# A gated attention and FFN block on one core: a rewritten opening, and h's first block maxima taken in the down stage

## What is computed

```python
def _quant_act(x2d, reorder_index, select_num):
    g = jnp.maximum(jnp.max(jnp.abs(x2d)) / GSCALE_DIV, 1e-08)
    xr = (x2d / g)[:, reorder_index]
    ...
    normal = _fp8_block_qdq(xr[:, :n])
    ...
    q1 = _fp8_block_qdq(outl)
    q2 = _fp8_block_qdq(outl - q1)
    return jnp.concatenate([normal, q1, q2], axis=1), g
def _L0_ffn_ref(x, w_gate, w_up, w_down, ri_in, ri_mid):
    A, g = _quant_act(x2, ri_in, SELECT)
    ...
    gate = A @ Wg.T * g
    up = A @ Wu.T * g
    h = jax.nn.silu(gate) * up
    Am, gm = _quant_act(h, ri_mid, SELECT)
    return Am @ Wd.T * gm
x = x + jnp.tanh(g_xattn[0]) * _L0_xattn_ref(_layernorm(x, axis=-1), ctx_4096, L0_xattn_x1_scale, L0_xattn_x1_zp, L0_xattn_x2_scale, L0_xattn_x2_zp)
x = x + jnp.tanh(g_ffn[0]) * _L0_ffn_ref(_layernorm(x, axis=-1), L0_ffn_w_gate, L0_ffn_w_up, L0_ffn_w_down, L0_ffn_ri_in, L0_ffn_ri_mid)
```

## Time and profile before

| what | us |
|---|---|
| median of 3 runs | 818.54 |
| the profiled execution's own time | 818.77 |
| its span, first to last instruction | 817.0 |
| PE busy in the span | 731.0 |
| DVE / ACT / POOL busy | 556.3 / 311.3 / 343.7 |
| loop and down stage on the chain that ended last | 387.38 + 224.48 |

### The profile page before, as it was taken

How to read it: one execution, slowest core, us unless ns; L and a number is a source line. 1 busy time by engine, 2 the same in 40 slices (tenths; PEclk the granted TensorE clock), 3 DMA queues, 4 the chain that set the end, 5 groups by cost and what they waited for, 6 DMA issues and landing times.

```text
span 817.0 us, 10350 instructions
## 1 busy us (share of the span) xinstructions
PE 731.0 (89%) x3473; PEld 334.5 (41%) x3473; DVE 556.3 (68%) x957; ACT 311.3 (38%) x382; POOL 343.7 (42%) x206
## 2 busy tenths in 40 slices
PE   0599003999999999999999999999999999999998
PEld 0144002545444444444444444444444444444443
DVE  5459789894475756675757575745898888988800
ACT  2798972445252524343434343430222122121100
POOL 1536766769374747584848575740000000000000
PEclk9989655999999999999999999999999999999999
DMA  8910598339588897979697969774265654555320
GB/s 308 353 60 14 166 279 147 80 64 190 145 173 212 187 211 174 223 169 227 145 232 163 231 163 236 157 157 164 49 152 162 182 129 149 132 161 121 88 60 26
DMA packets 228884, 131.56 MB, mean 161 GB/s; under 512 B 201712, under 2 KB 212976, under 8 KB 227824
## 3 DMA queue, kind: packets, MB, share of 16 engines
q1 hardware_dynamic: 228848, 131.12, 65.2%
HBM read 61.88 MB, written 19.66 MB: 100 GB/s over the span
## 4 chain that ended last, share of the span: by engine, by line
PE 78%; DVE 5%; POOL 5%; DMA 5%; ACT 3%; SPq 2%; issue 1%; DVEq 0%
PE acc L1276 47%; PE acc L1330 27%; DMA big<-in_ctx_dram 3%; PE acc L1223 2%; POOL big L739 1%; POOL h_in L734 1%; DVE big L1535 1%; ACT wbuf_all L919 1%; POOL wbuf_all L715 1%; POOL wbuf_all L708 1%; POOL big L728 1%; DMA wbuf_all<-in_L_ffn_w_up_dram 1%; SPq L455 1%; DMA mid<-big 1%; DMA x_d<-big 1%
## 5 line engine op out<-in xcount | busy, mean ns | idle before, releaser
L1276 PE MATMUL acc<-mid 128*128 128x512 f16 x1920 | 415.1, 379 | 0.0
L1276 PEld LDWEIGHTS acc<-mid 128*128 128x128 f16 x1920 | 187.9, 98 | 226.1
L1330 PE MATMUL acc<-big,mid 128*128 128x512 f16 x1040 | 224.6, 379 | 0.0
L818 POOL TENSOR_TENSOR h_in<-wbuf_all,h_in 128x1024 f16<-128x1024 f32 (+1 forms) x56 | 114.4, 2044 | 97.2 <-ACT h_in L1115 97.1
L1330 PEld LDWEIGHTS acc<-big,mid 128*128 128x128 f16 x1040 | 101.8, 98 | 122.7
L708 POOL TENSOR_TENSOR wbuf_all<-wbuf_all,w_inv 128x1024 f32<-128x1024 f32 (+1 forms) x67 | 125.2, 1873 | 43.6 <-DVE w_inv L1448 43.6
L1558 DVE SCALAR_TENSOR_TENSOR h_out<-acc,gs,silu 128x256 f32<-128x256 f32 (+1 forms) x88 | 41.5, 471 | 102.6 <-ACT silu L956 65.3
L1442 DVE TENSOR_REDUCE tb<-wbuf_all 128x64 f32<-128x1024 f32 (+1 forms) x67 | 78.9, 1178 | 47.3 <-DMA wbuf_all<-in_L_ffn_w_gate_dram 22.2
L912 ACT ACTIVATE wbuf_all<-wbuf_all 128x1024 f32<-128x1024 f32 (+1 forms) x67 | 68.1, 1016 | 82.2 <-POOL wbuf_all L708 81.4
L1115 ACT ACTIVATE h_in<-wbuf_all 128x1024 f16<-128x1024 f32 (+1 forms) x56 | 56.9, 1016 | 103.1 <-DVE wbuf_all L1454 103.1
L1454 DVE SCALAR_TENSOR_TENSOR wbuf_all<-wbuf_all,tb 128x1024 f32<-128x1024 f32 (+1 forms) x56 | 65.1, 1163 | 0.3 <-issue 0.2
(11 more groups left out here) (159 smaller groups left out, 555.0 us busy)
## 6 DMA issues: line engine op xcount, KB each, us to landing
h_in<-h_d SPq DMA_DIRECT2D x8, 1376.0 KB, 7.0
wbuf_all<-in_L_ffn_w_gate_dram SPq DMA_DIRECT2D x21, 512.0 KB, 4.3
wbuf_all<-in_L_ffn_w_up_dram SPq DMA_DIRECT2D x21, 512.0 KB, 4.3
h_d<-h_out SPq DMA_DIRECT2D x80, 128.0 KB, 3.5
...
```

What stands on the lines that cost most here:

```text
L818: last = pool.tensor_tensor(nat[s % 4][:, H:H + cols], wbuf[:, s % 4, 0:cols], nat[s % 4][:, 0:cols], ALU.subtract)
L1276: last = pe.matmul(acc[m % 4][:, 0:cols], left[:, k, s * P:(s + 1) * P], w[:, right, k, 0:cols], start=(k == 0 and left is a_hi and right ...
L1330: last = pe.matmul(acc[2 * i + hf][:], left[:, k - ks.start, :], right[:, k, hf * MW:(hf + 1) * MW], start=(k == 0 and left is hi and righ ...
```

## The change

**Opening.** The global maximum is gone. A tile's scales now come from its own row maxima (`coef_a`), since x1 is normalised with a fixed factor 2^10 and h is scaled by a fixed 2^-18; so each tile of A goes through on its own, in the groups 0-1, 2-5 and 6-7. `start_a` moves to POOL for all tiles (`start_pool`), the exponent is made on ACT in one instruction (`magic_a`), and its integer instruction on DVE is gone. `fold_outliers` is split in `fold_begin` and `fold_end`, with `magic_fold` on ACT between them; its work tile is now in SBUF instead of PSUM. Six weight pieces are scaled back on DVE in one instruction (`back_w`) in place of `whole_w` and `back_open`. Three of the eight `quantise_x` go to ACT. The row term is added in the down stage (`base`, on the loaded x1) in place of eight instructions of the opening. All ctx loads go ahead of the weight pieces. U pieces come before P pieces. The two waits of POOL for `ln_ready` are gone. The lists of all engines are written in a new order.

**Down stage.** For the opening's columns (0 to 255 and 2560 to 2751) `max_h` is gone; `open_max(t)` takes those maxima from the loaded tile, ahead of `row_scales(t)`.

The diff, cut to its core:

```diff
-OPENING = tuple((kind, t) for q in range(NT // 2) for kind in "PU" for t in (2 * q, 2 * q + 1))
+OPENING = (("U", 0), ("P", 0), ("P", 1), ("U", 1), ("U", 2), ("U", 3), ("P", 2), ("P", 3),
+           ("P", 4), ("U", 4), ("U", 5), ("P", 5), ("U", 6), ("P", 6), ("P", 7), ("U", 7))
...
+POOL_BACK = (0, 2, 3, 6, 7,)
...
-            lo_open(0)
-            back_open(1)
...
-            pool.wait_ge(ln_ready, 4)
...
+            start_pool(0)
+            lo_open(0)
+            lo_open(1)
+            start_pool(1)
...
+            def magic_a(t):
+
+                act.wait_ge(a_started[t], 1)
...
+                for hf in range(2):
+                    act.activation(tb[hf][:], xn_all[:, t, hf * MW:(hf + 1) * MW], ACT.Abs, scale=V_ABS).then_inc(a_magic, 1)
...
-            pe.wait_ge(part_max, 1)
-            spread_max(gmx[:, 0:1], tb[1][:, 0:P]).then_inc(all_max, 1)
...
+            pe.wait_ge(x1_ready, NT)
             pe.wait_ge(nat_a_lo, 1)
             for i in range(WARM):
                 pe.transpose(acc[3][:, 0:P], ident[:], ident[:])
-            for m in OPENING[0:2]:
-                multiply_open(m)
...
+            multiply_open(("U", 0))
+            for j in range(P_PIECES):
+                pe.wait_ge(piece_turned[buf(piece("P", j))], 16 * (piece("P", j) // 4 + 1))
+            multiply_open(("P", 0))
...
+            def coef_a(t):
+
+                dve.wait_ge(max_done, t + 1)
+                step(dve.tensor_reduce(a_top[:, t:t + 1], bmx[:, t, :], AX_X, ALU.max))
+                step(dve.tensor_scalar(a_low[:, t:t + 1], a_top[:, t:t + 1], TINY / GDIV, A_UP * TINY * TINY, ALU.mult, ALU.max))
+                step(dve.tensor_scalar(a_scale[:, t, :], bmx[:, t, :], 1.0 / FP8_MAX, a_low[:, t:t + 1], ALU.mult, ALU.max))
+                dve.reciprocal(bmx[:, t, :], a_scale[:, t, :]).then_inc(coef_ready, 1)
...
+            def back_w(n):
...
+                dve.scalar_tensor_tensor(out=w, in0=w, scalar=MAGIC, in1=spread(w_max[:, b, :]), op0=ALU.subtract, op1=ALU.mult)\
+                    .then_inc(w_back[b], 1)
...
+            def open_max(t):
+
+                i = t % 2
+                dve.wait_ge(h_loaded[i], 16 * (t // 2 + 1))
+                for a, z in ((0, UW), (NU * UW, I)):
+                    last = dve.tensor_reduce(hm[:, t, a // BLK:z // BLK], blocks(h_in[:, i, a:z]), AX_X, ALU.max,
+                                             apply_absolute_value=True)
+                step(last)
...
             last_h(0)
             last_h(1)
-            row_scales(0)
...
             last_h(2)
-            row_scales(1)
             last_h(3)
+            open_max(0)
+            row_scales(0)
             keep_h_outliers(0)
...
+            open_max(1)
+            row_scales(1)
             keep_h_outliers(1)
```

More of the change, by code:

```diff
@@ new lines, in _ @@
+            whole_w(2)
+            magic_a(1)
+            square_x1(5)
+            hi_open(2)
+            round_w(3, buf(3))
+            whole_w(3)
+            root(3, slice(2, 6))
+            round_w(4, buf(4))
+            norm(3, 2)
+            keep_outliers(2)
+            hi_open(3)
+            magic_fold(0)
+            norm(3, 3)
+            hi_open(4)
+            round_w(5, buf(5))
+            keep_outliers(3)
+            norm(3, 4)
+            hi_a(0)
+            hi_a(1)
@@ L1171, in _ @@
             magic_h(4)
+            base(0)
             for n in range(4, 2 * NT):
@@ L1616, in _ @@
             quantise_x(2)
-            make_x1(0)
-            layernorm(2, slice(4, NT), tt[:, 5:6], prm[:, 1:2])
+            first_stats(7)
+            aggregate(1, slice(4, 8))
             make_x1(1)
-            quantise_x(3)
-            quantise_x(4)
-            make_x1(2)
-            quantise_x(5)
+            layernorm(1, slice(4, 8), tt[:, 5:6], prm[:, 1:2])
+            spread_x1(2, slice(0, 2))
             col_lo(1)
             front_open(0)
+            make_x1(2)
+            front_open(1)
@@ L1626, in _ @@
+            layernorm(2, slice(0, 2), 2.0 * A_UP)
+            front_open(2)
+            max_a(0)
             quantise_x(6)
+            coef_a(0)
+            quantise_x(7)
             make_x1(3)
-            front_open(1)
             make_x1(4)
-            quantise_x(7)
-            spread_x1(3, slice(0, 4))
-            front_open(2)
+            back_w(1)
+            max_a(1)
+            coef_a(1)
+            end_a(0)
             make_x1(5)
-            layernorm(3, slice(0, 4))
             front_open(3)
-            max_a(0)
+            end_a(1)
@@ L1637, in _ @@
+            front_open(4)
+            spread_x1(3, slice(2, 6))
+            front_open(5)
+            layernorm(3, slice(2, 6), 2.0 * A_UP)
+            fold_begin(0)
+            max_a(2)
+            back_w(4)
+            front_open(6)
+            fold_end(0)
+            coef_a(2)
+            back_w(5)
+            max_a(3)
+            coef_a(3)
             make_x1(6)
-            max_a(1)
-            row_out()
-            max_a(2)
-            front_open(4)
             make_x1(7)
-            step(max_a(3))
@@ L1688, in _ @@
-            start_a(5)
             h_open(("P", 0))
-            h_open(("P", 1))
-            end_a(5)
-            h_open(("U", 0))
-            start_a(6)
+            layernorm(4, slice(6, 8), 2.0 * A_UP)
+            end_a(5)
+            max_a(6)
+            coef_a(6)
+            fold_begin(4)
+            h_open(("P", 1))
+            fold_end(4)
+            max_a(7)
+            coef_a(7)
+            h_open(("U", 1))
+            h_open(("U", 2))
             end_a(6)
-            fold_outliers(4)
```

827 lines of the change are left out of this document (402 added, 425 removed).

## The result

The changed kernel takes 807.53 us (median of four runs, 806.9 to 808.16) against 818.62 us for the kernel before on the same chip. The ratio is 0.9866, with a 95% interval of 0.9849 to 0.9883: about 11 us faster. The profiled execution took 806.9 us, its span is 805.1 us, so 11.9 us less than the span of before.

A forecast was written before the change was run, and what follows sets the result against it. TensorE (PE) was taken as the bound from 201.71 us on, so only its opening and staying fed count. Opening gain 15.2 us less down-stage cost 3.5 gives -11.7: 818.54 to 806.8 us, 8-in-10 range 789 to 815.

The forecast's parts named there:

- Start, 5.4 us: Opening: four weight pieces no longer ahead of ctx tiles, so front_open(0) begins at 56.4 instead of 61.76, 5.4 us earlier.
- VectorE's work, 41.0 us: Opening: VectorE's listed instructions up to the end of fold_end(0) sum to 41.0 us, without waits.
- Waits beside GpSimd, 15 us: Opening: 19 VectorE instructions wait 0.87 us each beside a GpSimd busy nine tenths of the time, 15 us.
- The 44% of the row: Opening: average wait per small VectorE instruction, 0.5 us beside GpSimd instructions of 1.13, read from the profile before.
- rival B: Opening: each of 19 VectorE instructions waits out a whole GpSimd instruction, 37 us instead of 15; 828.8 us, chance 0.07.
- To the first P tile, 133.3: Opening: from fold_end(0) at 112.4, through GpSimd's work and the last P piece's transpose, to the first P tile at 133.3.
- TensorE's 67.5 us: Opening: eight P tiles at 3.9 and seven U tiles at 5.18, 67.5 us; the loop's first unit starts at 200.8.
- The down stage, 3.5 us: Entry of the down stage: open_max and later row_scales delay lo_h, TensorE stalls 0.9 and 2.6 us, cost 3.5 us.
- Rival A: Opening: VectorE's waits beside GpSimd don't come; 791.8 us, or 789.0 with GpSimd as the bound; chance 0.2.
- rival C: Down stage: it loses nothing, because the first transposes land sooner than the median; 803.3 us, chance 0.1.
- rival D: Opening: A tiles or pieces come late to TensorE again and again, 15 us of stalls; 818 to 822 us, chance 0.03.

The follow-up runs named there:

- e13: The kernel before, with only the four first weight pieces put behind the last ctx tile on the queue: 813.31 us, ratio 0.9942.
- e11: The changed kernel with the four first weight pieces between ctx tiles 9 and 10, without the wait for the flags: 806.65 us, ratio 0.9857.
- The probe: The changed kernel with eight added small VectorE multiplications ahead of front_open(5), alternately two SBUF inputs or one in PSUM: 809.79 us, ratio 0.9897.
- e6: The changed kernel with GpSimd doing lo_open(5), lo_open(6) and lo_a(1) ahead of start_pool(3) and scale_a(2): 807.41 us, ratio 0.9872.
- e1: The changed kernel with the old down stage: sixteen max_h back in the opening, row_scales ahead of last_h(2) and last_h(3): 804.95 us, ratio 0.9845.

## Why the prediction was right, point by point

The time, 806.8 against 807.53, was right, and so were both of its parts, 15.2 and 3.5 us against 14.9 and 2.7. The mechanisms that it rests on, waits beside GpSimd and two stalls at the entry of the down stage, are in the trace. That it hit within 0.7 us is partly luck: steps 1 and 3 came to nearly the right number by another make-up, and the errors of steps 4 and 5 cancel.

1. *Start, 5.4 us: the number right, the cause half wrong.* `front_open(0)` was forecast at 56.4 and came at 56.80 (up to 58.16 in the other profiles with this order). In the kernel before the pieces did cost most of it (e13: 4.4 us). But I took a price out of the old opening and booked it in the new one, where it does not exist (e11). The two orders reach the same moment by different ways: the old one with ctx first, at 57.34, by earlier loads alone; the new one, at 56.80, with an attention that starts at 37.08, and with `make_x1(2)` moved behind `front_open(0)`.
2. *VectorE's work, 41.0 us: right.* From 56.80 to the end of `fold_end(0)` at 110.1 are 53.3 us; less the waits of 13.5, 39.8.
3. *Waits beside GpSimd, 15 us: the sum right, its make-up wrong.* I had 19 instructions at 0.87. Measured are nine that waited 0.7 to 1.9 us, 13.3 in sum (from 63.10 on in the rows above, each less what it takes alone: 0.16 on four columns, 0.65 for L1471, 1.16 for L1611, 0.37 and 0.42 in the fold), one of 0.2, and nine that did not wait. The 44% of the row was an average over three waits of 0.7 to 0.9 (of 1.13) and two of nothing, not the size of one; that the same average held in a new list is luck. The probe shows the single wait to be rival B's, what is left of a GpSimd instruction. The trace of before had one that rows 5 leave out, ending as GpSimd's L715 ends (72.43 and 72.41):

```profile
70.53 1.90 DVE L1379 TENSOR_SCALAR ve<-x_sq 128x4 f32<-128x4 f32 x1
```

That B did not come about is due to GpSimd's idle time: eight of the nine that did not wait began in it, the ninth (L1611 at 74.84) came 0.1 us before a GpSimd instruction ended. In part the waits make this time themselves: GpSimd's gaps of 2.86 and 2.25 us, before 100.32 and 104.69, end with ACT's fp16 halves, and ACT had stood 4.83 us for `layernorm(3)`'s factors and 1.88 for the `back_w` that took 3.03.
4. *To the first P tile, 133.3: 1.8 us too late.* `lo_a(0)` ended at 116.29 (117.7), `lo_open(6)` at 124.26 (126.7), because `fold_end(0)` ended 2.3 earlier; `start_pool(2)` took 0.8 longer than booked, and the wait of 0.87 did not come. The transpose then landed at 131.55, 7.3 us later instead of 6.6: SyncE issued it at 125.53, 1.3 us after it was ready, and e6 shows that an earlier piece would only have waited longer for SyncE.
5. *TensorE's 67.5 us: two us too short.* From 131.55 to 201.1 are 69.5: the first P tile took 5.74 instead of 3.9, at a granted clock of 0.70, and the second waited 0.2 for tile 1. The clock had stood at full speed through the 4.89 us of idle time and fell to the lower level from about 132 to 135 us. Rows 1 had shown that the first P tiles are slower (10.17 for two against 7.96), and the step priced all eight at 3.9. Later tiles came without a wait of TensorE. That cancelled step 4.

*The down stage, 3.5 us: 0.8 too much.* The two stalls were forecast at 0.9 and 2.6 and came at 0.82 and 1.85. The added work was as priced (`open_max` 0.67 in place of 0.77, `row_scales` 2.72 in place of 2.71). Against the forecast, shifted by the opening's 14.9, `lo_h(1)` ended 0.5 us sooner (586.19) and its transpose landed in 5.1 us instead of 5.2, and TensorE was free 0.1 later, which makes up the second stall's 0.7. What I said would cost nothing cost nothing: TensorE has no wait in the loop or in later tiles.

Rival A fell with the rows at 91.82 to 95.84; rival C with the 2.7 us of stalls at the entry, which e1 takes away; rival D with the timeline, in which one A tile waits 0.2 us.
